# Two spans of a convolution loaded and convolved earlier, and one weight tile's inverse scales computed alone

## What is computed

```python
out = conv_general_dilated(x, weight, ..., feature_group_count=4)
out = out + einsum('nd,od->no', c, c_weight)[:, :, None] + bias[None, :, None]

def fake_quant(t, axis):
    s = maximum(max(abs(t), axis=axis) / 127.0, 1e-8)
    return clip(round(t / s), -128, 127) * s

gate = qlinear(y, w_gate)          # w_gate, w_up: 1376 x 512
up = qlinear(y, w_up)
h = silu(gate) * up
return x + qlinear(h, w_down)      # w_down: 512 x 1376
```

## Time and profile before

| | |
|---|---|
| median of 3 runs | 282.3 us (282.22 to 282.36) |
| span of the profiled execution | 280.7 us |
| PE busy | 275.1 us |
| DVE busy | 243.5 us |
| ACT busy | 196.4 us |
| POOL busy | 207.4 us |

### The profile page before, as it was taken

The page is one execution under the profiler, slowest core; times in us unless marked ns, Lnnn a source line. Parts: engine busy times, 40 slices in busy tenths (PEclk is TensorE's granted clock), DMA queues, the critical chain, the costliest instruction groups (busy, mean ns, idle before and its releaser), DMA issues.

```text
span 280.7 us, 5318 instructions
## 1 busy us (share of the span) xinstructions
PE 275.1 (98%) x1862; PEld 153.6 (55%) x1862; DVE 243.5 (87%) x411; ACT 196.4 (70%) x237; POOL 207.4 (74%) x215
## 2 busy tenths in 40 slices
PE   8989999999999999999999999999999999999995
PEld 5978754454564464644444745744444444444443
DVE  0999999999999989799888679789988889888973
ACT  2269999989688886666888836726788886666820
POOL 1478999998969786866888836946778888667732
PEclk9999999999999999999999999999999999999999
DMA  7999923686929999646599992425456763334265
GB/s 268 406 420 419 377 69 71 129 200 171 223 61 221 249 212 238 190 126 187 145 244 296 218 271 77 128 53 128 126 156 163 151 176 98 94 88 124 51 142 187
DMA packets 81721, 51.62 MB, mean 184 GB/s; under 512 B 69664, under 2 KB 70560, under 8 KB 81568
## 3 DMA queue, kind: packets, MB, share of 16 engines
q1 hardware_dynamic: 81264, 50.84, 66.5%
q10 hardware_dynamic: 432, 0.46, 0.5%
HBM read 25.99 MB, written 8.39 MB: 122 GB/s over the span
## 4 chain that ended last, share of the span: by engine, by line
PE 85%; DMA 6%; DVE 4%; SPq 3%; issue 1%
PE bank L1305 52%; PE bank L1329 26%; PE bank L1207 6%; DMA h_mem<-w_gate_up 6%; DVE d_max L855 2%; SPq L352 1%; DVE gu_max L838 1%; SPq L340 1%; PE bank L1344 1%; DVE sg_mem L910 0%; PE bank L1231 0%; SPq L343 0%; DVE sg_mem L989 0%; SPq L329 0%; DVE gu_scale L845 0%
## 5 line engine op out<-in xcount | busy, mean ns | idle before, releaser
L1305 PE MATMUL bank<-wgu_t,xq_mem 128*128 128x512 bf16 (+1 forms) x768 | 154.8, 357 | 0.0
L544 POOL TENSOR_TENSOR sg_mem<-sg_mem,gu_scale_row 128x512 f32<-128x512 f32 (+1 forms) x96 | 110.9, 1162 | 36.3 <-ACT sg_mem L702 36.2
L1305 PEld LDWEIGHTS bank<-wgu_t,xq_mem 128*128 128x128 bf16 x768 | 73.7, 98 | 73.2 <-DVE h_mem L923 1.6
L702 ACT ACTIVATE sg_mem<-sg_mem,x_scale 128x512 f32<-128x512 f32 (+1 forms) x96 | 62.7, 672 | 30.0 <-DVE sg_mem L910 29.5
L1329 PE MATMUL bank<-wd_t,hq_mem 128*128 128x512 bf16 (+1 forms) x341 | 78.2, 379 | 0.0
L923 DVE SCALAR_TENSOR_TENSOR h_mem<-bank,x_scale,sg_mem 128x512 f32<-128x512 f32 (+1 forms) x96 | 65.7, 691 | 8.9 <-POOL sg_mem L544 8.2
L910 DVE TENSOR_TENSOR sg_mem<-bank,gu_scale_row 128x512 f32<-128x512 f32 (+1 forms) x96 | 59.7, 626 | 9.4 <-PE bank L1305 9.2
L707 ACT ACTIVATE h_mem<-h_mem,h_inv 128x1376 f32<-128x1376 f32 (+1 forms) x32 | 45.3, 1419 | 28.2 <-DVE h_inv L831 28.2
L1329 PEld LDWEIGHTS bank<-wd_t,hq_mem 128*128 128x128 bf16 (+1 forms) x341 | 33.4, 98 | 39.6
L928 DVE TENSOR_REDUCE h_max<-h_mem 128x1 f32<-128x1376 f32 x31 | 48.8, 1576 | 0.0
L715 ACT ACTIVATE hq_mem<-h_mem 128x1376 bf16<-128x1376 f32 (+1 forms) x32 | 42.0, 1314 | 0.2
(11 more groups left out here) (71 smaller groups left out, 175.2 us busy)
## 6 DMA issues: line engine op xcount, KB each, us to landing
xo_mem<-x SPq DMA_DIRECT2D x24, 256.0 KB, 3.0
out<-xo_mem SPq DMA_DIRECT2D x24, 256.0 KB, 2.2
hq_mem<-w_gate_up SPq DMA_DIRECT2D x7, 512.0 KB, 10.9
slab_taps<-x_slabs SPq DMA_DIRECT2D x6, 512.0 KB, 5.5
slab<-x_slabs SPq DMA_DIRECT2D x6, 512.0 KB, 8.7
slab_taps<-w_down SPq DMA_DIRECT2D x3, 688.0 KB, 14.2
h_mem<-w_gate_up SPq DMA_DIRECT2D x4, 512.0 KB, 15.8
slab_taps<-x SPq DMA_DIRECT2D x1, 2048.0 KB, 9.8
```

The lines of the kernel that those rows point to most:

```text
L544: pool.tensor_tensor(s, s, gu_scale_row[:, 1, at:at + n], ALU.mult).then_inc(silu_scaled, 1)
L702: act.activation(s, s, ACT.Silu, scale=x_scale_of(i)).then_inc(silu_done, 1)
L1305: last = pe.matmul(bank[n % 2][:, 0:cols], xq_t[:, g, k, P * c:P * (c + 1)], wgu_t[:, m, k, at:at + cols], start=(k == 0), stop=(k == KT - 1))
```

## The change

Three moves, on three engines. On SP, the load of the sixth pair of spans goes ahead of the load of the fifth weight tile. On DVE, the inverse scales of the first weight tile and of the second are each computed right behind their scales, in place of one instruction for both further down. On PE, `conv_pair(5)` goes ahead of `turn_xq(0)` and `turn_xq(1)`. Nothing else differs.

```diff
             load_pair(4)
             load_w(2)
             load_w(3)
+            load_pair(5)
             load_w(4)
-            load_pair(5)
             load_w(5)
@@ DVE
             weights_top(0)
             fold_y(3)
             weights_scale(0, 1)
+            weights_inverse(0, 1)
             weights_top(1)
             add_shift(6)
             weights_scale(1, 1)
+            weights_inverse(1, 1)
             add_shift(7)
-            weights_inverse(0, 2)
             fold_y(5)
@@ PE
             run_empty(up_bank[1], 6)
             turn_gate_up(1)
+            conv_pair(5)
             turn_xq(0)
             turn_xq(1)
-            conv_pair(5)
             turn_gate_up(2)
```

## The result

The changed kernel takes 283.03 us (median of 8 runs, 282.94 to 283.7), the kernel before 282.35 (8 runs): ratio 1.003, 95% interval 1.0021 to 1.0039. It is slower by 0.68 us. I had forecast 282.5 and 282.0 to 283.0.

What follows compares the result with a forecast made beforehand. Bound: when TensorE enters its dense stretch at turn_down_row (38.84 us), plus its work behind. TensorE 0.60 later less 0.36 slack gave +0.24, taken as +0.2: 280.9 + 1.6 = 282.5 us, range 282.0 to 283.0.

Steps and rivals of the forecast that it cites:

- GpSimd's first round: GpSimd's rounding of the first weight tile, round_w(0), forecast to start at 14.1 us instead of 15.53.
- TensorE's new gap ahead of `turn_gate_up(2)`: TensorE idle for 1.0 us while it waits for round_w(2), whose inverse comes 0.46 us late.
- The chain over ScalarE that I named as the price: Later scale rows delay ScalarE's copies and round_y by 0.83 us, so the banks for conv_pair(6) come free later.
- PE is 0.60 us later from here: TensorE at conv_pair(6): forecast to start at 24.65 instead of 24.05, delayed by 0.60 us from there on.
- 39.08 instead of 38.84: +0.24: Forecast start of turn_down_row: TensorE ready at 38.48 + 0.60 = 39.08, so 0.24 us later than before.
- The chain from `conv_pair(5)` to `conv_pair(6)`: Forecast from conv_pair(5) at 17.9, over the scale rows and ScalarE's copies, to conv_pair(6) at 24.65.
- The start of `conv_pair(5)`: On TensorE behind turn_gate_up(1): forecast at 17.9 us, when its load is just in.
- the reserve: Slack of 0.36 us on TensorE ahead of turn_down_row, where it waited for d_scale; VectorE had 0.36 too.
- Rival 1: Nothing reaches the end: TensorE's delay stays under its 0.36 us of slack, time 282.3; chance 0.17.
- Rival 2: Slower: conv_pair(5) waits for its own load, some +0.7 us, 283.0; chance 0.12.
- Rival 3: Slower: ScalarE's lateness of 0.6 us comes through behind 39 us, up to +0.6 more, 283.1; chance 0.05.
- Rival 4: Slower: TensorE's new 1.0 us gap drops its clock to 1.2 GHz, a guessed +2 us; chance 0.02.

Runs made afterwards that it cites:

- e1_pe_back: Changed kernel with conv_pair(5) back behind turn_xq(0) and turn_xq(1), load and inverses still moved: 282.31 us against 282.38 for the kernel before.
- e6_split_only: Kernel before with only the two inverses moved: 282.53 us against 282.59 for the kernel before.
- e5_after_again: Changed kernel itself, unaltered, run again beside the kernel before: 283.34 us against 282.59.
- e4_load_earlier: Changed kernel with load_pair(5) one place further forward, ahead of load_w(3): 283.28 us against 282.38 for the kernel before.
- e2_no_split: Changed kernel with only the inverses undone, one instruction for both tiles where it was: 285.56 us against 282.38 for the kernel before.
- e13_act_and_load: Changed kernel with copy_xq(1) moved behind copy_span(11) and load_pair(5) ahead of load_w(3): 282.97 us against 282.41 for the kernel before.

## Why the prediction was wrong

**What held.** The mechanism, and the size of most steps. GpSimd's first round came at 14.19 for 14.1, the inverse with its scale took 0.27 for 0.28, `d_scale` came 0.10 late as forecast (38.62 for 38.52), TensorE's new gap ahead of `turn_gate_up(2)` is shown with 0.77 us for 1.0, the wait for the ninth tile vanished (in the second profile one of 0.33 us for the eighth stands in its place), and `turn_down_row` stopped waiting. The chain over ScalarE that I named as the price is the one the trace shows, and e1_pe_back with e6_split_only shows that TensorE's move is the whole price, to within 0.3 us.

**What failed.** The term "PE is 0.60 us later from here", in the sum "39.08 instead of 38.84: +0.24", was too small. It measured 1.01 (24.05 to 25.06) in the changed kernel's profile and 1.12 in its second. It has two mis-sized parts.
- The chain from `conv_pair(5)` to `conv_pair(6)`: I worked out 24.65 - 17.9 = 6.75, the five profiles with ScalarE's order unaltered show 6.87 or 6.88. This is 0.12 us. Half lies ahead of `round_y(0)`, which starts 3.81 us behind `conv_pair(5)` (18.19 to 22.00) for 3.75, and half in the step from the end of `copy_span(11)` to `conv_pair(6)`: 0.14 (24.92 to 25.06) for 0.08.
- The start of `conv_pair(5)`: 17.9 in my sum, 18.19 and 18.29 in two profiles, so 0.29 and 0.39 us late. In the first it was the load, forecast to land at 17.8 and landed at 18.15 (5.94 + 12.21); without it the start would have been 17.99. In the second it was the opening: `conv_pair(4)` started at 14.44, and `conv_pair(5)` follows it by 3.85 or 3.86 us in the four profiles that have TensorE's move and the early inverses and show no hold by the load of pair 5. I took the opening of the one execution that I had, with `conv_pair(4)` at 13.99, as fixed. In the 14 profiles it started at 13.58 to 14.96, with a median of 14.4, in seven of them behind a wait for its own load.

For the first profile the sum closes: 0.60 + 0.12 + 0.29 = 1.01, and `turn_down_row` starts at 39.48 instead of 38.84, +0.64, where 0.24 + 0.12 + 0.29 is 0.65. For the usual execution an estimate from the median opening is 14.4 + 3.85 = 18.25, 0.35 late, and 0.24 + 0.12 + 0.35 = 0.71 us; measured are 0.68 and 0.75. That closeness is in part luck: the estimate keeps 38.84 for the kernel before, and in e1_pe_back and e6_split_only `turn_down_row` started at 38.91 and 38.99, by which it would be about 0.1 less. No run forced the opening, so its share over many runs is argued and not shown. Nor do the times speak for it: on the chip of e5_after_again the changed kernel's full-clock runs lie between 282.85 and 283.53, those of the kernel before between 282.08 and 282.92, no wider spread without the reserve than with it.

**The rivals.** Rival 1 (nothing reaches the end) fell. Rival 2 named the right point, the start of `conv_pair(5)`, and its sign is there: the chain of the first profile begins with that load. It also named 283.0, which was measured; that is a coincidence, since the load's part is 0.20 us in one profile, and moving it out of the way (e4_load_earlier) gains nothing. Rival 3 did not occur: the 112 matmuls take 22.02 us in both, and from 39 us on TensorE's weight loads wait for VectorE for 2.7 us in all, against 2.8 before. Rival 4, the clock, was priced at +2 by a guess and given 0.02; two of 20 runs of the changed kernel fell to it, at +1.6 and +1.95 us over the median of their group, and with TensorE 0.9 us later at that point five of six. It is not in the 0.68: the eight runs of the result all have a mean clock of 0.998 or more.

## What to carry to other kernels

An instruction moved ahead of another on a busy engine pays on the queue of whoever reads the second one; follow that queue to the next thing it frees, here two banks behind five other instructions of ScalarE. One profile of the kernel before shows a single draw of how early its loads land and its opening runs; where a change uses up a reserve to within some tenths of a microsecond, the start it counts from needs a range of its own. (That the reserve had hidden this variation is my reading; the spread of the times does not show it.) An engine that is full has no place to put displaced work, and what it wins ahead of a stretch it may lose behind.

## What the runs showed of the hardware

TensorE's granted clock fell from 2.4 to 1.2 GHz inside a kernel that keeps it 97% busy (e2_no_split), behind a stretch in which it had been busy for 2.05 of 4 us and no gap shown was longer than 0.97 us, and was back within 4 us. The 36 small float32 matmuls of one pair took 3.85 us instead of 2.23, and the execution some 2 us more. Whether it fell differed from run to run of the same kernel: five of six runs, two of twenty, or one of twelve (e13_act_and_load). In the profile of e5_after_again TensorE was busy for 2.12 of the 4 us from 22 to 26, hardly more than the 2.05, and the clock stayed up. With empty matmuls in the gaps it stayed up in all six runs.

Two 512 KB loads that changed places on one queue changed the order of their landings: pair 5 at 18.15 and the fifth weight tile behind it, at 19.35, where the tile had landed at 17.8 and pair 5 at 19.1.
